# A graph-attention kernel on Trainium2: the edge loop's reach found in units of 125 edges, its step and ring cut from four to three

## The reference

```python
dst = jnp.minimum((1250 * jax.random.uniform(fold_in(_gk, 3), (20000,)) ** 2.0).astype(jnp.int32), 9999)
_o = jnp.argsort(dst, stable=True)
src = src[_o]; dst = dst[_o]
...
xn = _layernorm(x)
x1 = relu(xn @ W_ah + b_ah)
e = leaky_relu(as_n[src] + ad_n[dst]); p = exp(e - m[dst])      # three attention layers of 4 heads, edges + loops
out = segment_sum(alpha * h[src], dst)
x = x + gnn(xn) + linear_attention(xn)
x = x + routed_ffn(_layernorm(x))
```

## Time and profile before

| | |
|---|---|
| median of 3 runs | 1473.88 us (1471.35 to 1474.57) |
| the profiled execution's own time | 1471.52 us |
| its span | 1468.9 us |
| mean granted TensorE clock | 0.977 of full |
| PE busy | 1371.9 us, 93% |
| DVE busy | 1064.0 us, 72% |
| the counting loop, PE's first L596 to the end of `front` | 119.81 to 268.55 us |

### The profile page before, as it was taken

How to read it: one execution, slowest core, us unless ns; L and a number is a source line. 1 busy time by engine, 2 the same in 40 slices (tenths; PEclk the granted TensorE clock), 3 DMA queues, 4 the chain that set the end, 5 groups by cost and what they waited for, 6 DMA issues and landing times.

```text
span 1468.9 us, 21232 instructions
## 1 busy us (share of the span) xinstructions
PE 1371.9 (93%) x8204; PEld 1287.8 (88%) x8204; DVE 1064.0 (72%) x1966; ACT 490.1 (33%) x813; POOL 36.5 (2%) x41
## 2 busy tenths in 40 slices
PE   4999899899999788897999999999999999999886
PEld 4965566899999688897999999999999999999875
DVE  6867988699999732466677577767767776778666
ACT  2310122234344410333432433243334324333363
POOL 2100000000000022000000000000000000000000
PEclk9999999999999899998999999999999999999998
DMA  8410000222221373710110120111011011104003
GB/s 225 156 65 0 2 1 1 68 68 85 86 86 54 90 239 111 200 67 1 35 39 1 68 73 1 68 36 38 1 68 42 32 47 45 52 1 137 1 0 105
DMA packets 23428, 91.58 MB, mean 62 GB/s; under 512 B 3549, under 2 KB 4672, under 8 KB 20397
## 3 DMA queue, kind: packets, MB, share of 16 engines
q1 hardware_dynamic: 22417, 88.06, 18.8%
q10 hardware_dynamic: 924, 2.30, 0.6%
HBM read 79.29 MB, written 11.06 MB: 62 GB/s over the span
## 4 chain that ended last, share of the span: by engine, by line
PE 50%; DVE 7%; ACT 2%; issue 1%; DVEq 0%
PE psum L1617 24%; PE psum L101 8%; PE psum L102 8%; PE psum L103 8%; DVE prob L1247 1%; DVE prob L1241 1%; DVE hN L1263 1%; PE psum L1631 1%; ACT prob L1454 1%; PE psum L1671 1%; DVE acc L1372 0%; PE psum L1656 0%; ACT xn L1500 0%; DVE x1l L1270 0%; DVE wpl L1289 0%
## 5 line engine op out<-in xcount | busy, mean ns | idle before, releaser
L1617 PE MATMUL psum<-hN,prob 125*125 125x193 f32 x2400 | 412.5, 328 | 10.0 <-DVE hN L1263 7.6
L1617 PEld LDWEIGHTS psum<-hN,prob 125*125 125x125 f32 x2400 | 398.3, 189 | 11.0 <-issue 10.8
L1454 ACT ACTIVATE prob<-prob,acol 125x1250 f32<-125x1250 f32 x120 | 160.9, 1341 | 391.7 <-DVE prob L1241 391.6
L1247 DVE SCALAR_TENSOR_TENSOR prob<-prob,cnt 125x1250 f32<-125x1250 f32 x120 | 174.7, 1456 | 71.8 <-ACT prob L1454 71.8
L1241 DVE SCALAR_TENSOR_TENSOR prob<-vrow,ncol,urow 125x1250 f32<-125x1250 f32 x120 | 181.7, 1515 | 3.4 <-PE psum L1617 3.4
L704 DVE CUSTOM_DVE_ANT_0 junk<-mask,arow 125x1250 bf16<-125x1250 uint8 x120 | 174.8, 1456 | 3.1
L101 PE MATMUL psum<-woh,xlh 128*125 128x384 f32 x360 | 128.2, 356 | 2.6 <-DVE acc L1285 2.6
L101 PE MATMUL psum<-wph,x1h 128*125 128x384 f32 x330 | 118.7, 360 | 8.9 <-DVE x1l L1270 8.9
L102 PE MATMUL psum<-wol,xlh 128*125 128x384 f32 x360 | 123.9, 344 | 0.0
L596 PE MATMUL psum<-hot_src,hot_dst 125*125 125x416 bf16 (+1 forms) x588 | 115.7, 352 | 8.2 <-DVE hot_src L426 8.1
L103 PE MATMUL psum<-woh,xll 128*125 128x384 f32 x360 | 123.1, 342 | 0.0
(11 more groups left out here) (219 smaller groups left out, 2214.2 us busy)
## 6 DMA issues: line engine op xcount, KB each, us to landing
arow<-scratch_a SPq DMA_DIRECT2D x12, 625.0 KB, 3.9
urow<-scratch_uv SPq DMA_DIRECT2D x12, 625.0 KB, 4.3
vrow<-scratch_uv SPq DMA_DIRECT2D x12, 625.0 KB, 5.8
wq_raw<-in_w_qkv SPq DMA_DIRECT2D x6, 1152.0 KB, 6.9
wp_raw<-in_w_pair SPq DMA_DIRECT2D x6, 1152.0 KB, 7.7
wo_raw<-in_w_out SPq DMA_DIRECT2D x6, 1152.0 KB, 5.9
wl<-in_w_gat SPq DMA_DIRECT2D x4, 1152.0 KB, 7.2
xN<-in_x SPq DMA_DIRECT2D x10, 336.0 KB
```

The lines of the kernel that those rows point to most:

```text
L1247: nc.vector.scalar_tensor_tensor(prob[n % RING][:, :], prob[n % RING][:, :], 1.0, cnt[:, n % NT, :], op0=ALU.min, op1=ALU.mult).then_inc(p ...
L1454: nc.scalar.activation(prob[n % RING][:, :], prob[n % RING][:, :], ACT.Exp, bias=acol[:, n // NT, n % NT:n % NT + 1]).then_inc(e_ready, 1)
L1617: last = nc.tensor.matmul(bank(t // 2)[0:P, 193 * (t % 2):193 * (t % 2) + 193], ring[:, t * P:(t + 1) * P], hN[i % 2][:, j, 193 * s:193 * ...
```

## The change

The reach of a node group is found in single units of 125 edges in place of chunks of 500. The loops on DVE and PE start at the group's first unit and go on in steps of three. The ring of one-hot tiles has three places. `src_f` and `dst_f` get two columns more (the last step may pass the end), of which `dst_f`'s hold -1, a node that no group has. The lowest and highest nodes are now 160 numbers each, computed on 80 partitions as pairs of units, written with one DMA and read back with two.

```diff
-CE = 4
-CHUNKS = ET // CE
+CE = 3
+HALF = ET // 2
-    dram_ends = scratch("ends", (CHUNKS, 2))
+    dram_ends = scratch("ends", (2, ET))
...
-        chunk_f = at("chunk_f", MASK_AT + 2048, [CHUNKS, CE * P])
+        chunk_f = at("chunk_f", MASK_AT + 2048, [HALF, 2 * P])
...
-            sp.dma_start(g["dram_ends"], ends[:, :]).then_inc(ends_in, 16)
+            sp.dma_start(g["dram_ends"].rearrange("e (c u) -> c e u", u=2), ends[:, :, :]).then_inc(ends_in, 16)
             sp.wait_ge(ends_in, 16)
-            sp.dma_start(ends_bc[:, :, :], g["dram_ends"].partition_broadcast(NT)).then_inc(ends_in, 16)
+            for k, row in enumerate((lowest_in, highest_in)):
+                sp.dma_start(row[:, :], g["dram_ends"][k].partition_broadcast(NT)).then_inc(ends_in, 16)
...
-                    own.done(nc.vector.tensor_copy(src_f[:, :], src_i[:, :]))
-                    own.done(nc.vector.tensor_copy(dst_f[:, :], dst_i[:, :]))
-                    own.done(nc.vector.tensor_reduce(ends[:, 0:1], chunk_f[:, :], axis=AX.X, op=ALU.min))
-                    nc.vector.tensor_reduce(ends[:, 1:2], chunk_f[:, :], axis=AX.X, op=ALU.max).then_inc(ends_ready, 1)
+                    own.done(nc.vector.tensor_copy(src_f[:, 0:ET], src_i[:, :]))
+                    own.done(nc.vector.tensor_copy(dst_f[:, 0:ET], dst_i[:, :]))
+                    own.done(nc.vector.memset(src_f[:, ET:ET + CE - 1], 0.0))
+                    own.done(nc.vector.memset(dst_f[:, ET:ET + CE - 1], -1.0))
+                    units_of = chunk_f[:, :].rearrange("c (u p) -> c u p", u=2)
+                    own.done(nc.vector.tensor_reduce(ends[:, 0, :], units_of, axis=AX.X, op=ALU.min))
+                    nc.vector.tensor_reduce(ends[:, 1, :], units_of, axis=AX.X, op=ALU.max).then_inc(ends_ready, 1)
...
-            dve.wait_ge(ends_in, 32)
-            own.done(nc.vector.tensor_scalar(in_reach[:, :], ends_bc[:, :, 0], start[:, 1:2], None, ALU.is_lt))
+            dve.wait_ge(ends_in, 48)
+            own.done(nc.vector.tensor_scalar(in_reach[:, :], lowest_in[:, :], start[:, 1:2], None, ALU.is_lt))
...
-                with dve.Fori(first, final) as c:
+                with dve.Fori(first, final, CE) as unit:
                     for e in range(CE):
...
-                                                dst_f[:, bass.ds(c * CE + e, 1)], None, ALU.is_equal)\
+                                                dst_f[:, bass.ds(unit + e, 1)], None, ALU.is_equal)\
...
-                with pe.Fori(first, final):
+                with pe.Fori(first, final, CE):
```

More of the change, by code:

```diff
@@ L181, in front @@
         prod = at("prod", MASK_AT + 4096, [128, C])
-        chunk_i = at("chunk_i", MASK_AT, [CHUNKS, CE * P], I32)
-        chunk_f = at("chunk_f", MASK_AT + 2048, [CHUNKS, CE * P])
+        chunk_i = at("chunk_i", MASK_AT, [HALF, 2 * P], I32)
+        chunk_f = at("chunk_f", MASK_AT + 2048, [HALF, 2 * P])
         node_i = at("node_i", X1_AT, [P, N], I32)
@@ L198, in front @@
         src_i, dst_i = at("src_i", Z, [P, ET], I32), at("dst_i", Z + 640, [P, ET], I32)
[L199 to L203, removed]
+        src_f, dst_f = at("src_f", Z + 1280, [P, ET + CE - 1]), at("dst_f", Z + 1952, [P, ET + CE - 1])
+        wa = at("wa", Z + 2624, [128, KT, 2 * HEADS])
+        node_id = at("node_id", Z + 3200, [P, N], FP16)
+        eye = at("eye", Z + 5728, [P, 2 * N - P], BF16)
+        a_blk = at("a_blk", Z + 10496, [128, KT, 2 * HL])
         low = sb("low_a", [HEADS, 1])
-        ends = sb("ends", [CHUNKS, 2])
-        ends_bc = sb("ends_bc", [NT, CHUNKS, 2])
+        ends = sb("ends", [HALF, 2, 2])
         start_i, start = sb("start_i", [NT, 1], I32), sb("start", [NT, 2])
-        chunk_no_i, chunk_no = sb("chunk_no_i", [NT, CHUNKS], I32), sb("chunk_no", [NT, CHUNKS])
-        in_reach = sb("in_reach", [NT, CHUNKS])
+        unit_no_i, unit_no = at("unit_no_i", MASK_AT + 1024, [NT, ET], I32), at("unit_no", MASK_AT + 3072, [NT, ET])
+        lowest_in, highest_in = at("lowest_in", MASK_AT + 11264, [NT, ET]), at("highest_in", Z + 10688, [NT, ET])
+        in_reach = at("in_reach", MASK_AT + 1024, [NT, ET])
         reach_f, reach = sb("reach_f", [NT, 2]), sb("reach", [NT, 2], I32)
@@ L301, in _ @@
             nc.gpsimd.iota(start_i[:, :], pattern=[[0, 1]], base=0, channel_multiplier=P).then_inc(const_ready, 1)
-            nc.gpsimd.iota(chunk_no_i[:, :], pattern=[[1, CHUNKS]], base=0, channel_multiplier=0).then_inc(const_ready, 1)
+            nc.gpsimd.iota(unit_no_i[:, :], pattern=[[1, ET]], base=0, channel_multiplier=0).then_inc(const_ready, 1)
             own.done(nc.gpsimd.memset(ident[:, :], 0.0))
@@ L416, in _ @@
             for w in range(NT):
-                first = dve.value_load(g["reach_row"][0:1, 2 * w:2 * w + 1], min_val=0, max_val=CHUNKS - 1)
-                final = dve.value_load(g["reach_row"][0:1, 2 * w + 1:2 * w + 2], min_val=1, max_val=CHUNKS)
-                with dve.Fori(first, final) as c:
+                first = dve.value_load(g["reach_row"][0:1, 2 * w:2 * w + 1], min_val=0, max_val=ET - 1)
+                final = dve.value_load(g["reach_row"][0:1, 2 * w + 1:2 * w + 2], min_val=1, max_val=ET)
+                with dve.Fori(first, final, CE) as unit:
                     for e in range(CE):
@@ L423, in _ @@
                         nc.vector.tensor_scalar(hot_dst[:, e, 0:P], node_id[:, w * P:(w + 1) * P],
-                                                dst_f[:, bass.ds(c * CE + e, 1)], None, ALU.is_equal)\
+                                                dst_f[:, bass.ds(unit + e, 1)], None, ALU.is_equal)\
                             .then_inc(hot_ready, 1)
-                        nc.vector.tensor_scalar(hot_src[:, e, :], node_id[:, :], src_f[:, bass.ds(c * CE + e, 1)],
+                        nc.vector.tensor_scalar(hot_src[:, e, :], node_id[:, :], src_f[:, bass.ds(unit + e, 1)],
                                                 None, ALU.is_equal).then_inc(hot_ready, 1)
@@ L588, in _ @@
                                             stop=False, skip_group_check=True)
-                first = pe.value_load(g["reach_row"][0:1, 2 * w:2 * w + 1], min_val=0, max_val=CHUNKS - 1)
-                final = pe.value_load(g["reach_row"][0:1, 2 * w + 1:2 * w + 2], min_val=1, max_val=CHUNKS)
-                with pe.Fori(first, final):
+                first = pe.value_load(g["reach_row"][0:1, 2 * w:2 * w + 1], min_val=0, max_val=ET - 1)
+                final = pe.value_load(g["reach_row"][0:1, 2 * w + 1:2 * w + 2], min_val=1, max_val=ET)
+                with pe.Fori(first, final, CE):
                     for e in range(CE):
@@ L1774 @@
         "dst_t": a["dst"].reshape(ET, P).T,
-        "dst_c": a["dst"].reshape(CHUNKS, CE * P),
+        "dst_c": a["dst"].reshape(HALF, 2 * P),
         "w_ah": a["L0_gnn_W_ah"].reshape(KT, 128, KT, 128).transpose(2, 1, 0, 3),
```

16 lines of the change are left out of this document (8 added, 8 removed).

## The result

| | before | after |
|---|---|---|
| median | 1471.49 us (1469.48 to 1474.57, 14 runs) | 1468.05 us (1466.11 to 1469.26, 14 runs) |
| profiled execution | 1471.52 us, span 1468.9 | 1466.94 us, span 1464.7 |
| front ends | 268.55 us | 264.88 us |

The ratio is 0.9976, with a 95% interval of 0.9969 to 0.9983: 3.5 us less, where 3.7 were forecast. (The time itself was forecast as 1469.7 us; the median of before, which that started from, was of three runs and lay 2.4 us above the one of fourteen.) In the kernel after, the lines of interest have moved by four (L423 is L427, L426 is L430, L596 is L600, L409 is L413), those of the layer norm by one (L345 is L346).

The account below looks back on a forecast made before the run. DVE's unit pace and its restart by PE in each group bound the loop. Groups +1.86 - 1.85 - 3.70 = -3.7 us, all else 0: 1467.8 from the profiled execution, 1470.2 from the median; forecast 1469.7, range 1465.5 to 1474.5 us.

Parts of the forecast that it names:

- The group's length, 0.90 + 0.6175 x (units - places) + 3.66: Loop: PE start to DVE restart, DVE's remaining units, then tail to the next group; 9.50 us for 12 units, four places.
- Rival 1: Loop: only units count and a missing place costs nothing; -9.9 us, 1464 us; chance 0.06.
- The ring of three: Loop: a turn of three places takes 1.67 us against 1.85 us available, so it costs 0.
- rival 2: DVE's L423 within a group: turn exceeds 1.85 us; 0.07 over takes the gain, 0.2 over gives 1476 us; chance 0.17.
- Group 1, -1.85: Loop's second node group: four units fewer, one place less, DVE one unit behind until PE is fast again; -1.85 us.
- Groups 0 and 2 to 8: Loop, (change of units + 1) x 0.6175: group 0 +1.86 us; then -0.62, 0, 0, -1.85, +0.62, +0.62, -1.23.
- a return: DVE's loop returns: passes grow from 49 to 60; 11 more cost between 0 and 0.1 us, taken as 0.
- Group 9, -1.23: Last node group of the loop: -1.23 us, its tail being the end of `front`, the same before and after.
- rival 3: Clock falls inside groups as PE starves earlier; some 1.3 us a fall, three falls take the gain; chance 0.08.
- The front, 0: Ahead of the loop: DVE reaches L345 some 0.5 us earlier, but POOL's L311 holds it; 0, bounds -0.86 and 0.
- The reach: Finding each group's units: wider DVE instructions, 1.3 us at most, and 0.3 on SP, covered by later waits; taken as 0.
- DVE's idle at a group's start, 1.9: Loop: DVE's wait for PE at each group's start was to rise from 1.24 to about 1.9 us.

Follow-up runs that it names:

- the lead of three: Kernel before, chunks and four places kept, with DVE allowed three units ahead of PE in place of four: 1479.37 us, ratio 1.0062.
- its repeat: Kernel before with DVE three units ahead, plus 32 register moves that did not reach the trace, so the same instructions: 1479.83 us.
- the two with memsets: Kernel before with DVE three units ahead, plus eight or twenty-four unused memsets ahead of DVE's loops: ratios 1.0057 and 1.0048.

## Why the prediction held, step by step

- **The group's length, 0.90 + 0.6175 x (units - places) + 3.66**: right. Group 6 has all three terms, and the lead of three shows the price of a place by itself (+0.65 to +0.70 in groups 2 to 8). Rival 1, that only units count, is dead: 12-unit groups took 10.1 to 10.3 us, not 9.5.
- **The ring of three** (rival 2): does not bind at the full clock; the turn is 1.67 us, as summed. The time given with this rival holds a slip: the +6.3 us of a turn of 2.05 was added to the forecast, which already holds the gain. From before it would have come to some 1478 to 1480 us, not 1476.
- **Group 1, -1.85**: mis-sized by 1.0 us. The step that failed is that DVE "stays one unit behind until PE is fast again", as if PE were slow over the same stretch as before. It was not: PE worked at the low level for 5.8 us in place of 3.4. Windows of PE in before, then in after (behind PE's busy time: clock, DMA share, GB/s):

```profile
156.20:157.00 0.80, 0.80 (x5) 0.87 0.00 0
...
160.20:160.80 0.60, 0.60 (x5) 1.00 0.00 0
```

```profile
156.00:156.85 0.85, 0.00 (x1) 0.50 0.51 71
...
162.60:163.20 0.60, 0.60 (x5) 0.95 0.00 0
```

  Before, PE started the group at 155.46 with the full clock, which fell near 156.8 and was back at 160.20: 3.4 us at 1.2 GHz. After, it was down before PE started at 156.85 and came back near 162.6: 5.8 us of PE's work. In that time three places tie DVE to PE, and its L427 comes every 1.04 us:

```profile
160.39 0.26 DVE L427 TENSOR_SCALAR hot_dst<-node_id,dst_f 125x125 bf16<-125x125 f16 x1 [0.33 <-PE psum L600]
161.43 0.26 DVE L427 TENSOR_SCALAR hot_dst<-node_id,dst_f 125x125 bf16<-125x125 f16 x1 [0.33 <-PE psum L600]
```

  DVE's eleventh unit starts 8.43 us after its first (156.08 to 164.51); before, 6.80 (154.69 to 161.49). That is 1.63 us more, where one unit, 0.62, was forecast: the missing 1.0. With four places in single units the clock was low from about 154.8 to 158.2 only, and the group came out at -2.45 for -2.47; with five it was low from ahead of the start until about 161.9, and 1.05 us were missing. The kernel with five places and the edge block moved settles that the places are not the cause. It has the same loop, its clock was low from 155.4 to 158.8, and its group 1 took 18.33 us, all of the 2.5 us, where the other took 19.38. Windows of group 1, five places, then with the block moved:

```profile
155.93:175.31 19.38, 18.61 (x89) 0.85 0.00 0
```

```profile
155.20:173.53 18.33, 17.55 (x90) 0.91 0.00 0
```

  And over a low stretch like that of before, a missing place costs what I took for it: the three later kernels with a lead of three (its repeat and the two with memsets), whose PE worked 3.2 to 3.4 us of group 1 at the low level, have +0.59 to +0.62. So the forecast of -1.85 needed the low stretch of before. In ten of the thirteen traces it begins 126.3 us behind the change of pace in the first product (30.50 to 156.79 in before, 29.54 to 155.83 in after), and so at another distance from PE's restart in each. Why, and why it lasts 3.4 us in some and 6.8 in others, is open.
- **Groups 0 and 2 to 8**: right within 0.2 us each. Group 5 lost 0.12 to a late return (L427 at 216.75 and 217.47, 0.72 us apart), the kind that the memsets moved; a return else left no mark, as taken.
- **Group 9, -1.23**: measured -1.66. The step "its tail is the end of `front`, the same before and after" failed. It is not an effect of the change: two executions of the same instructions differ there too (1.62 and 1.78 us, above). Before, the ten matmuls of the last turn ran at a mean clock of 0.69 and took 2.29 us; after, in as long a stretch at 1.00, 1.62. Windows of before and then of after, from 4 us ahead of the front's end:

```profile
264.50:268.50 4.00, 2.29 (x10) 1.87 (x10) 0.87 (x2) 2.58 (x6) 0.00 (x0) 0.69 0.00 0
```

```profile
260.80:264.80 4.00, 1.62 (x10) 1.24 (x10) 1.32 (x2) 2.93 (x7) 0.00 (x0) 1.00 0.01 4
```

- **The clock in groups 2 to 9** (rival 3): stayed at 1.00 in the loop. It was lower only at the start of group 1 (in after already within PE's idle of 3.50 us), and (before, not after) in the last turn, behind an idle of 1.70.
- **The front, 0**: right in its reason. DVE's block is 1.89 us for 2.29 (two memsets of 0.06 each, for 0.15 taken), DVE comes to L346 0.28 earlier, and L346 ends at 22.29, 0.42 behind POOL's end at 21.87; PE's first product starts at 25.10, where before it is 25.00. The prediction took from 33.16 against 33.20 that L345 pays where it meets L311; by the starts of these rows DVE is 0.04 us ahead there and pays all the same, so that row does not show that the later one blocks. Where L345 comes 1.1 us behind POOL, as here, it does pay. The 0.37 us by which the loop starts earlier come from PE's pace in its first product. One window of PE in before, then in after:

```profile
30.00:31.00 1.00, 1.00 (x5) 1.00 0.00 0
```

```profile
30.00:31.00 1.00, 1.00 (x9) 1.00 0.92 43
```

  In this microsecond PE does nine matmuls in after and five in before, from nearly the same start, and the fifth tile's `xnl` comes at 31.67 for 32.06. A matmul of 418 columns starts every 0.35 us up to 30.4 in before and up to 29.4 in after, and every 0.19 us from there. The 0.35 is the pace of the loop's matmuls at clock 0.50 (1.04 us for three). The clock column has 1.00 here in both, but that is no reading: the traces' records of the clock begin only at 30.50 and 29.54, where the pace changes. So this is in all likelihood the clock's rise from its 1.2 GHz level. I had expected 119.81 for the loop's start in the lead of three and 119.44 with four places, if the front's edit was what moved it; they came at 120.05 and 118.98. In the thirteen traces the change lies anywhere from 28.5 to 31.1 us, so the 0.37 us lie well within what changes without any edit.
- **The reach**: covered, as taken. DVE's first one-hot comes at 98.99 for 98.61, and then waits 19.39 us for PE.
- **DVE's idle at a group's start, 1.9**: measured 1.36 to 1.48. The place that is missing splits the wait: 0.36 us of it now lies ahead of the first unit that DVE makes for the next group. The sum was not touched by it.

So the number came out closer than its working. The loop gave -3.30 us for -3.70, with two errors of opposite sign (+1.0 and -0.4), both where the granted clock differs from the kernel before; the loop's start, which I had at nothing, gave -0.37 by what looks like chance. That the end of `front` moved by 3.67 us is luck to that extent (the medians differ by 3.5, the profiled executions by 4.6). What is shown is the price of a unit and of a place in the groups that run at the full clock.

## What to carry to other kernels

A ring between two engines costs as often as it is drained: count how many times the consumer's first unit restarts the producer, and price each missing place at the producer's unit time for each restart; the rounding of the loop's step is paid in the same coin, so write both as one sum before choosing the step. Check then that the ring's turn fits into its places at the lowest clock at which the consumer may run, not only at the full one. Where two engines hold each other up, look who starts first and by how much: an edit that makes one of them earlier by a few tenths can give nothing or all of it. And before a microsecond is put down to an edit, look whether two executions of the same instructions agree in it; here they differed by 1.0 us in the loop's start.

## What the hardware did that I had not expected

- Around PE's idle of some 3.5 us ahead of group 1, the granted clock fell 1.3 us after PE's restart in one kernel and ahead of it in another, and stayed at 1.2 GHz for 3.4 or 5.8 us of PE's work. Two executions of after agreed in this within 0.1 us. Two executions of the lead of three's instructions did not: the fall came 0.5 us ahead of the restart in one and 1.6 behind it in the other.
- PE's first product changed from 0.35 to 0.19 us a matmul at 28.5 to 31.1 us, and the first record of the clock in each trace lies there. Each us of it moves the loop's start by some 0.45 us (2.28 us and 1.00 between the two executions of the lead of three).
- Ten matmuls at the end of `front` took 1.62, 2.29 or 2.66 us in kernels that are alike there, by the clock granted over them (1.00, 0.69, 0.50).
- DVE's L345 against POOL's L311: with a row start 0.03 to 0.05 us ahead DVE takes 2.3 us and POOL its plain 1.85; with 0.11 to 0.13 us ahead DVE takes its plain 0.68 and POOL 2.24.
- Matmuls whose tiles are addressed by a register: a unit of three every 1.44 us within a pass and every 1.8 over its return, at clock 0.50 and 1.00 alike, for 0.62 with fixed addresses (there DVE sets the pace).
- DVE's loop return is late in some loops by 0.10 us at each return (group 0 of the lead of three) or 0.16 once (groups 4 and 8 with the memsets), and which loop it is goes with the number of instructions ahead.
